# Inverse roots of the third layer norm on GpSimd by Newton steps, and a later place for a block's rows, logits and ranks

## The reference

```python
x = x + delta_rule_attention(_layernorm(x))     # a scan over the tokens, 16 heads
x = x + moe_ffn(_layernorm(x))                  # 8 experts, top 2, 640 slots an expert
x = x + linear_attention(_layernorm(x))         # features, 16 heads of 8, 128 features each
x = x + moe_ffn(_layernorm(x))                  # the same experts again
```

```python
q_p = elu(einsum('bhnd,hdf->bhnf', q, proj)) + 1.0
attn = einsum('bhnf,bhfd->bhnd', q_p, kv) / (q_p . k_sum)
x = x + attn @ W_out.T + b_out
...
def _layernorm(x, axis=-1, eps=1e-05):
    return (x - m) / jnp.sqrt(v + eps)
...
logits = xt @ w_g
top_v, top_i = jax.lax.top_k(logits, TOP_K)
exp_rank = jnp.cumsum(exp_mask.reshape(TOP_K * T, N_EXP), axis=0) - 1   # its slot in the expert
```

## Time and profile before

| | |
|---|---|
| median of 3 runs | 561.44 us (560.64 to 562.64) |
| the profiled execution: its time, its span | 562.72 us, 561.0 us |
| PE, DVE, ACT, POOL busy over the span | 70%, 52%, 43%, 44% |
| query features and routing | about 348 to 461 us of the span |
| experts and the sum, after them | 461 to 561 us |
| chain that ended last, by engine | PE 43%, DVE 11%, issue 7%, DMA 5%, ACT 4%, POOL 3% |

### The profile page before, as it was taken

The page is one execution under the profiler, slowest core; times in us unless marked ns, Lnnn a source line. Parts: engine busy times, 40 slices in busy tenths (PEclk is TensorE's granted clock), DMA queues, the critical chain, the costliest instruction groups (busy, mean ns, idle before and its releaser), DMA issues.

```text
span 561.0 us, 6660 instructions
## 1 busy us (share of the span) xinstructions
PE 392.6 (70%) x2204; PEld 256.3 (46%) x2204; DVE 289.1 (52%) x679; ACT 239.8 (43%) x360; POOL 248.6 (44%) x289
## 2 busy tenths in 40 slices
PE   4768676556540599999078999778676309999950
PEld 1354343333230388888045333234343207888840
DVE  6466788888622021411285999867767201222203
ACT  2476554343240243232136998774945212323210
POOL 5077766889644946464331000001441641555550
PEclk9969888656655599999669999976967558999985
DMA  4237382880047221210524444500100121121108
GB/s 123 82 89 252 119 271 80 254 243 21 25 141 225 72 68 56 71 56 27 136 62 99 99 99 96 182 1 5 34 24 14 43 82 28 55 80 53 52 31 224
DMA packets 45748, 52.94 MB, mean 94 GB/s; under 512 B 6417, under 2 KB 28561, under 8 KB 45713
## 3 DMA queue, kind: packets, MB, share of 16 engines
q1 hardware_dynamic: 36304, 41.73, 25.7%
q0 software_dynamic: 4608, 8.47, 4.4%
q10 hardware_dynamic: 4800, 2.30, 1.6%
HBM read 26.11 MB, written 21.12 MB: 84 GB/s over the span
## 4 chain that ended last, share of the span: by engine, by line
PE 43%; DVE 11%; issue 7%; DMA 5%; ACT 4%; POOL 3%; POOLq 0%; ACTq 0%; DVEq 0%
PE ps L1129 39%; DVE feat L1055 4%; POOL slots_x L442 3%; DMA got<-chosen_y 2%; PE ps L1265 2%; DMA slots_x<-rows_x,put_at 1%; ACT expo L718 1%; DMA xe<-slots_x 1%; DMA chosen_y<-ye,y_to 1%; POOL chosen_y L490 1%; PE ps L1222 1%; ACT L718 1%; DVE stats L854 1%; ACT xnT L507 1%; PE ps L1374 0%
## 5 line engine op out<-in xcount | busy, mean ns | idle before, releaser
L442 POOL DMA_INDIRECT slots_x<-rows_x,put_at x64 | 63.1, 986 | 149.6 <-DVE put_at L902 131.4
L490 POOL DMA_INDIRECT chosen_y<-ye,y_to x80 | 78.2, 977 | 85.6 <-DVE ye L996 63.9
L615 ACT ACTIVATE hT<-ps 128x640 f32<-128x640 f32 x64 | 45.1, 704 | 98.7 <-issue 62.0
L1055 DVE SCALAR_TENSOR_TENSOR feat<-expo,ps 128x1024 f32<-128x1024 f32 x64 | 76.9, 1218 | 11.9 <-ACT expo L718 9.8
L1129 PE MATMUL ps<-xeT,cfc_sb 128*128 128x320 f32 x256 | 75.9, 452 | 1.8 <-DVE xeT L974 1.8
L718 ACT ACTIVATE expo<-ps,minus_one 128x1024 f32<-128x1024 f32 x64 | 70.2, 1114 | 13.3 <-PE ps L1129 9.5
L1129 PE MATMUL ps<-cproj_sb,hT 128*128 128x128 f32 x640 | 74.6, 275 | 0.3
L1129 PEld LDWEIGHTS ps<-cproj_sb,hT 128*128 128x128 f32 x640 | 73.0, 192 | 0.9 <-ACT hT L615 0.6
L974 DVE COPY xeT<-ps 128x640 f32<-128x640 f32 x16 | 13.2, 825 | 99.5 <-PE ps L1265 56.5
L1129 PEld LDWEIGHTS ps<-xeT,cfc_sb 128*128 128x128 f32 x256 | 47.9, 200 | 24.0 <-ACT hT L615 6.5
L433 POOL TENSOR_TENSOR read<-state,qT 128x512 f32<-128x512 f32 x32 | 40.9, 1279 | 22.9 <-DVE state L823 16.5
(11 more groups left out here) (201 smaller groups left out, 594.4 us busy)
## 6 DMA issues: line engine op xcount, KB each, us to landing
decay<-k_rows SPq DMA_DIRECT2D x32, 256.0 KB, 4.7
stk<-part SPq DMA_DIRECT2D x96, 64.0 KB, 2.0
slots_x<-empty_rows SPq DMA_DIRECT2D x16, 325.0 KB, 6.0
xe<-slots_x SPq DMA_DIRECT2D x16, 325.0 KB
chosen_y<-empty_rows SPq DMA_DIRECT2D x16, 256.0 KB
cfc_sb<-in_L_ffn_c_fc SPq DMA_DIRECT2D x2, 2048.0 KB, 8.9
got<-chosen_y SPq DMA_DIRECT2D x8, 256.0 KB, 5.5
got<-chosen_y ACTq DMA_DIRECT2D x8, 256.0 KB, 6.4
```

The source lines that it names most:

```text
L442: pool.indirect_dma_start(out=slots_x[k], out_offset=bass.IndirectOffsetOnAxis(ap=put_at[:, c, kk, t:t + 1], axis=0), in_=rows_x[:, kk * N ...
L490: pool.indirect_dma_start(out=chosen_y[k], out_offset=bass.IndirectOffsetOnAxis(ap=y_to[:, b, i:i + 1], axis=0), in_=ye[:, b, i * D:(i + 1 ...
L615: act.activation(hT[:, b, f, :].rearrange("p (a n) -> p a n", a=2), ps[:, 2 + 2 * (f % 2):4 + 2 * (f % 2), 0:HALF], ACT.Gelu).then_inc(h_r ...
L1055: dve.scalar_tensor_tensor(out=feat[:, g % 4, :], in0=expo[:, g % 3, :], scalar=1.0, in1=flat(ps[:, pair, :]), op0=ALU.min, op1=ALU.max).t ...
```

## The change

Three things change. The blocks 0 to 2 of this norm no longer use ACT's square root and DVE's `ln_scale`; POOL makes the inverse root itself, with an integer first guess and three Newton steps, 17 instructions on 4 columns, each of which waits for the one before. Block 3 keeps the old way. `ln_rows` of a block stood behind unit 7 of the next block and now stands two units later, behind unit 1 of the block after that; for block 2 this is behind the last unit and its `copy_at`. In blocks 2 and 3 the ROUTE slot moves from behind unit 1 to behind unit 3, the RANK slot from behind unit 3 to behind unit 6.

```diff
 def unit_slot(c, u):
-    return 8 * c + u + max(0, c - 1) + 2 * max(0, c - 2) + (u > 4) * (c >= 1) + ((u > 1) + (u > 3)) * (c >= 2)
+    return 8 * c + u + max(0, c - 1) + 2 * max(0, c - 2) + (u > 4) * (c >= 1) + ((u > 3) + (u > 6)) * (c >= 2)
...
-ROUTE_AT = {unit_slot(c + 2, 1) + 1: c for c in range(NB - 2)}
-RANK_AT = {unit_slot(c + 2, 3) + 1: c for c in range(NB - 2)}
+ROUTE_AT = {unit_slot(c + 2, 3) + 1: c for c in range(NB - 2)}
+RANK_AT = {unit_slot(c + 2, 6) + 1: c for c in range(NB - 2)}
...
             def experts(k):
                 for c in range((NB - 2) * (1 - k), NB):
                     for j in range(2 * TB):
+                        if k == 1 and c == 0 and j == TB:
+                            inverse_root(2)
                         scatter(k, c, j)
...
+            def link_root(ins):
+                root_steps[0] += 1
+                ins.then_inc(root_step, 1)
+                pool.wait_ge(root_step, root_steps[0])
+
+            def inverse_root(c):
+                tt = slice(TB * c, TB * c + TB)
+                pool.wait_ge(ln_mv[4], tiles_past(4) + TB * (c + 1))
+                link_root(pool.tensor_scalar(var_eps[:], mv[:, tt, 1], EPS, None, ALU.add))
+                link_root(pool.tensor_scalar(guess[:].bitcast(I32), var_eps[:].bitcast(I32), -0.5, float(0x5F3759DF),
+                                             ALU.mult, ALU.add))
+                link_root(pool.tensor_scalar(half[:], var_eps[:], 0.5, None, ALU.mult))
+                y = guess[:]
+                for it in range(3):
+                    new = rstd[:, tt] if it == 2 else guess[:]
+                    link_root(pool.tensor_tensor(y_sq[:], y, y, ALU.mult))
+                    link_root(pool.tensor_tensor(y_sq[:], y_sq[:], half[:], ALU.mult))
+                    link_root(pool.tensor_scalar(y_sq[:], y_sq[:], -1.0, 1.5, ALU.mult, ALU.add))
+                    link_root(pool.tensor_tensor(new, y_sq[:], y, ALU.mult))
+                link_root(pool.tensor_scalar(half[:], mv[:, tt, 0], -1.0, None, ALU.mult))
+                pool.tensor_tensor(shift[:, tt], half[:], rstd[:, tt], ALU.mult).then_inc(root_ready, 1)
...
+            inverse_root(0)
+            inverse_root(1)
             experts(1)
...
             def ln_rows(n, c):
-                act.wait_ge(ln_shift[n], shifts_past(n) + c + 1)
+                if n == 4 and c < NB - 1:
+                    act.wait_ge(root_ready, c + 1)
+                else:
+                    act.wait_ge(ln_shift[n], shifts_past(n) + (c + 1 if n == 2 else 1))
...
                     if u == 5:
                         copy_at(c, 0)
-                        if c:
-                            ln_root(4, c - 1)
-                    if u == 7 and c:
-                        ln_rows(4, c - 1)
+                    if u == 1 and c >= 2:
+                        ln_rows(4, c - 2)
...
             copy_at(NB - 1, 1)
+            ln_rows(4, NB - 2)
             turned_rows(4, NB - 2, 0)
...
-                    if u == 6 and c:
-                        ln_scale(4, c - 1)
```

More of the change, by code:

```diff
@@ L97, in program @@
         shift = sb("shift", [P, NT])
+        var_eps = sb("var_eps", [P, TB])
+        guess = sb("guess", [P, TB])
+        y_sq = sb("y_sq", [P, TB])
+        half = sb("half", [P, TB])
         wg_sb = sb("wg_sb", [P, NE])
@@ L239, in program @@
         stored = sem("stored")
+        root_step, root_ready = sem("root_step"), sem("root_ready")
         N_CONST = 8
@@ L493, in experts @@
                             oob_is_err=False).then_inc(ye_out[b], 16)
+            root_steps = [0]
+            def link_root(ins):
[18 more added lines that the diff above has]
+                pool.tensor_tensor(shift[:, tt], half[:], rstd[:, tt], ALU.mult).then_inc(root_ready, 1)
             experts(0)
@@ L862, in ln_scale @@
                 mean = mv[:, tt, 0] if moments is None else moments[:, :, 0]
-                dve.wait_ge(ln_std[n], blocks_past(n) + c + 1)
+                done = blocks_past(n) + (c + 1 if n < 4 else 1)
+                dve.wait_ge(ln_std[n], done)
                 dve.reciprocal(rstd[:, tt], std[:, tt]).then_inc(ln_rstd[n], 1)
-                dve.wait_ge(ln_rstd[n], blocks_past(n) + c + 1)
+                dve.wait_ge(ln_rstd[n], done)
                 dve.scalar_tensor_tensor(out=shift[:, tt], in0=mean, scalar=-1.0, in1=rstd[:, tt],
```

## The result

The changed kernel takes 557.61 us (556.06 to 558.71, 4 runs), the one before beside it 561.53 us (560.64 to 562.64, 4 runs): a ratio of 0.9922, interval 0.9898 to 0.9945, 3.9 us less. The forecast was 561.0. Its profiled execution took 558.71 us, with a span of 556.9, so 4.1 us of span are to be found.

What follows compares the result with a forecast made beforehand. The stage's end was taken to hang on POOL's scatter queue: features 9.4 us earlier, POOL losing 9.0 to the root and the scatters behind it, net -0.4 us, so 561.0 us, range 557.5 to 566.5 for 8 in 10.

Steps and rivals of the forecast that it cites:

- The loads and the root, removed: ACT's table loads and root gone: unit 2.0 starts about 3.7 us earlier, 2.6 us more gained in blocks 2 and 3.
- The moved logits (`choose`): DVE, block 2: `choose` hidden before `add_b`; 1.80 + 2.9 - 1.0 (logits) - 1.0 (rows) = 2.7 us gained.
- the sum: Features: 6.4 us earlier at `add_b` of block 1, 3.0 more to block 2's, together 9.4 us.
- S: How much earlier block 2's moments come: 9.4 us, at about 409.7.
- The root on POOL: 17 dependent POOL instructions at 0.30 us a step, R = 5.1 us, range of steps 0.25 to 0.43.
- Where the gain goes: POOL's queue from block 2's moments to its first scatter: 24.7 us for 15.7, losing 9.0 against 9.4 gained.
- (1): Rival: PE stays at its faster rate, S = 11.5, -2.5 us, 558 to 559; chance 0.28.
- the slow case: Bound on the features: PE at the slow rate all through, some 1.5 us more in each block, S 6 to 7.
- (2): Rival: POOL's root steps cost more, deciding from about 0.42 us a step; 564 to 569, chance 0.18.
- (3): Rival: features gain less, S = 6.5, PE slow and slots choking the banks; +2.5 us, 564, chance 0.14.

Runs made afterwards that it cites:

- e2: Kernel before with the new ROUTE and RANK slots and the later `ln_rows`, roots still on ACT: 557.19 us, ratio 0.9890 to 0.9960.
- e11: Kernel before with only the ROUTE and RANK slots moved, `ln_rows` still behind unit 7, on another chip than e7: 558.34 us, ratio 0.9896 to 0.9971.
- e3: Changed kernel with block 2's root made 17 linked POOL products longer, results unused: 562.06 us, ratio 0.9965 to 1.0027.
- e4: Changed kernel with block 2's root issued behind all eight of block 0's scatters: 551.73 us, ratio 0.9740 to 0.9852.
- e6: e4 with block 2's `ln_rows` ahead of the last `copy_at` on ACT: 554.96 us, ratio 0.9854 to 0.9925.
- e7: Kernel before with only the ROUTE and RANK slots moved, `ln_rows` still behind unit 7: 563.06 us, ratio 0.9977 to 1.0048.
- e9: The same kernel as e4, timed again on another chip against the kernel before: 554.06 us, ratio 0.9812 to 0.9888.
- e10: The same kernel as e6, timed again on another chip against the kernel before: 550.58 us, ratio 0.9763 to 0.9851.

## Why the prediction was wrong, point by point

- **"The loads and the root, removed"** was right in block 2. The first feat instruction of block 2 starts 4.73 us behind block 0's moments, 8.46 before: 3.73 for a forecast of 3.7.
- **"The moved logits (`choose`)"** is the step that failed, and by its size. It gave 2.7 us net in block 2: 1.80 + 2.9, with 1.0 off for the logits' wait and 1.0 for the rows. From unit 2.0's feat to `add_b` of block 1 the time fell from 15.27 to 10.33, 4.94. Three things make up about the 2.2 us that were missed: the logits' wait was 0, the rows cost DVE 0.60, the short wait at 377.31, and the way from unit 2.3's feat to `add_b` shrank from 4.89 us to 3.96, where the term left it as it was (it had taken block 3's 5.4 us, at PE's slower rate). In block 3, from `add_b` to `add_b`, 3.64 was gained for a forecast of 3.0, with no wait for the logits, 1.18 us of waiting at 396.14, where the exponential behind the rows ended, and 0.97 at `add_b`, with PE at the slower rate. Block 2's moments came 12.3 us earlier (both from block 0's), where the sum had S = 9.4. `add_b` of block 2 was at 404.58, for the 407 to 411 that the prediction gave as a sign.
- **What hid this** is that I took each wait as something that would partly come back behind the next unit. In the changed kernel, and in e2 and e11 as well, `choose` and a unit, 4.0 us from 380.68 to 384.69, lie over attend, turn and out_b, which take 3.8 us or less at PE's faster rate, so the waits go whole; at the slower rate 0.97 us is left. The order alone gives 8.0 us, where its terms in the sum came to 2.7 + 0.4 = 3.1 (in block 3, 3.0 without the 2.6 for the loads).
- **The two parts don't add as written.** The removed loads and roots are 3.7 + 2.6 = 6.3 us in my sum. On top of the order they gave 4.35 (41.18 to 36.83), and alone 2.3. The order's terms were too small by 4.9 us, and the loads' too large by 2.0; the difference is the 2.9 by which S was missed.
- **The root on POOL** was right: 0.28 us a step for 0.30, 4.76 us from 406.55 to the end of `shift` at 411.31 for 5.1. The page of the Trainium skill "Perfetto Trace Analysis", section "GPSIMD Engine Instruction", wants start-to-start spacing, and by that rule the step is 0.28 where the instruction's own span is 0.19 to 0.25. "GPSIMD Engine Reference", section "When to use GPSIMD", speaks against the place; by the runs the root's work isn't dear, but e2 against the changed kernel (557.19 for 557.61) shows that it bought nothing where it stood.
- **"Where the gain goes"** was right in kind and near in size: 25.21 us for 24.7. The second landing took 2.93 instead of 2.15, and 0.51 us passed behind the root for 0.3. put_at of block 2 was ready 7.8 us before POOL came to it, for 7. e3 confirms it, and e4 confirms its reverse: without four scatters and a landing in that queue the time falls by 3.5 to 6 us.
- **The rivals.** The side and nearly the size of (1) came, 557.61 for its 558 to 559, and its cause is seen in part: after, attend takes 1.06 us in block 2's chain but 1.94 in block 3's, with a granted clock of 0.91 over the stretch. The rate is worth about 0.9 us a block (after against e4) and doesn't carry the gain: e4, with the faster rate in both chains, has S = 13.2 (49.14 - 35.95), above the 11.5 that (1) took for the fast rate, and the changed kernel with one slow chain has 12.3, where the slow case was put at 6 to 7. That the time came out by (1)'s figure is thus partly luck. (2) fell with steps of 0.28 us, and (3) with S at 12.3.
- **Not expected at all** was that the whole change is worth what its order alone is. The root gains 4.35 us in the features and loses 4.1 in POOL's queue (25.21 for 21.15).

Open stay the longer landing, and the waits of 3 to 4 us that e6 and e7 had. Whether these come with the chip, the time of the run or the placement of the program was not separated.

## What to carry to other kernels

When work moves from a busy engine to one that has slack, count from its start what already stands in that engine's queue behind it, and put it behind what is ready and ahead of what isn't: here the place of one line was worth 3.5 to 6 us, and the move itself nothing. When independent work is put into a wait, compare its length with that of the chain waited for, at each rate the rows show: here 4.0 us of DVE's work hid a chain of at most 3.8 us whole, and left 0.97 us of one of 4.9. And try the parts of a change apart and again on another chip, since one set of runs of the slots alone read as nothing and the next as 3.4 us.

## What the runs showed of the hardware

Seventeen linked POOL instructions on 128x4 cost 0.27 to 0.33 us each from start to start, 0.28 for most, whether they read one operand or two. The first guess, on the bits as integers, is no exception: 370.06 to 370.33 in block 0's root of the changed kernel.

Executions of one kernel are mostly shorter where the granted clock over the whole execution is higher (not always: e6 has 553.6 us at 0.810 and 557.6 at 0.816). e9's six are 551.4 and 552.0 us at 0.820 and 553.9 to 555.5 at 0.801 to 0.806; the kernel before takes 559.4 to 562.9 us at 0.807 to 0.813 and 564.2 to 566.6 at 0.788 to 0.803. e4's four runs all had 0.816 or 0.820, and at 0.820 it takes 550.6 and 551.4, so that its 551.7 and e9's 554.1 are mostly one kernel in different mixtures. A difference of 3 us between two kernels of few runs is only as good as that mixture.

DVE can wait 3 to 4 us at one place in one set of runs (e6, e7) and not at all in another (e10, e11) of the same kernel, with no releaser in the trace, and with such waits the medians of one kernel lie 4.7 us apart (563.06 and 558.34). The clock doesn't explain this: at 0.810 to 0.813 e7 takes 561.6 to 563.3 us and e11 556.5 to 558.4.
